# Shared network: seven blocks in the first route and one in retention's opening, gathers reordered, the last group power among block 0's scatters

## The reference, cut to what matters

```python
x = x + time_mix(layernorm(x))     # RWKV recurrence over time
x = x + ffn(layernorm(x))          # first expert layer
x = x + retention(layernorm(x))    # 16 heads, per batch of 1024 tokens
x = x + ffn(layernorm(x))          # second expert layer, the same weights
# ffn(x): 64 experts of 64 hidden, top 4 per token, weighted by a softmax
routed = einsum('ne,nef,efd->nd', comb, silu(x @ wg) * (x @ wu), wd)
shared = (silu(x @ swg) * (x @ swu)) @ swd     # 2 networks of 256 hidden
return routed + shared
# retention: scores = (q k^T) * decay, ret = scores v; group norm over a
# head's whole sequence; out = (silu(x wg) * norm(ret)) wo + bo
```

## Time and profile before

| what | value |
|---|---|
| median of 3 runs | 1552.0 us (1551.07 to 1554.17) |
| the profiled execution's own time | 1554.0 us |
| its span, first to last instruction | 1552.3 us |
| granted TensorE clock, mean | 0.911 of full |
| PE, DVE, POOL, ACT busy | 82%, 71%, 63%, 44% of the span |
| time_mix | up to about 184 us |
| moe1: route, expert pairs | to about 402 us, to about 600 us |
| retention: opening, rest | 604 to 692 us, to about 1005 us |
| moe2: route, expert pairs, sums | to about 1197 us, to about 1484 us, to 1552 us |

### The profile page before, as it was taken

One profiled execution on the slowest core, in us unless ns is written; L12 is line 12 of the kernel. 1 busy time (PEld: TensorE's weight loads), 2 busy tenths in 40 slices (PEclk: granted clock), 3 DMA queues, 4 the chain that ended last, 5 costly groups with the idle time before them and its releaser, 6 DMA issues. The chain is left out here.

```text
span 1552.3 us, 24686 instructions
## 1 busy us (share of the span) xinstructions
PE 1267.0 (82%) x7408; PEld 874.9 (56%) x7408; DVE 1098.7 (71%) x2756; ACT 687.5 (44%) x1464; POOL 984.6 (63%) x1308
## 2 busy tenths in 40 slices
PE   7788567998599997999898998389998887787751
PEld 3344444665488884556565766246655665665521
DVE  5899887776266664557687878567773777787758
ACT  6999421221366664234333441222211765665610
POOL 4999668888555554775665514287884566676710
PEclk9899768999799998999999899779999999999966
DMA  9900162223688786412021100182325655554178
GB/s 356 414 36 0 30 283 101 96 104 119 213 270 281 261 286 216 124 43 79 29 72 41 56 1 33 30 351 81 105 98 148 199 178 177 171 180 137 45 284 298
DMA packets 109399, 233.83 MB, mean 151 GB/s; under 512 B 21544, under 2 KB 43471, under 8 KB 108757
## 3 DMA queue, kind: packets, MB, share of 16 engines
q1 hardware_dynamic: 81076, 164.03, 31.6%
q0 software_dynamic: 27648, 68.23, 12.9%
q10 hardware_dynamic: 544, 0.00, 0.0%
HBM read 125.44 MB, written 115.11 MB: 155 GB/s over the span
## 5 line engine op out<-in xcount | busy, mean ns | idle before, releaser
L978 POOL DMA_INDIRECT slots_x<-arena,slot x240 | 250.5, 1044 | 42.9 <-POOL slot L931 33.4
L1342 POOL DMA_INDIRECT pairs_y<-arena x192 | 189.4, 986 | 109.4 <-DVE arena L1413 54.3
L762 PE MATMUL moe_wide<-arena 128*128 128x512 f32 x416 | 198.2, 623 | 17.7 <-DVE arena L1091 17.7
L1259 PE MATMUL moe_narrow<-arena 128*128 128x128 f32 x1536 | 211.2, 282 | 0.0
L1259 PEld LDWEIGHTS moe_narrow<-arena 128*128 128x128 f32 x1536 | 194.4, 199 | 1.5 <-issue 1.0
L1405 DVE TENSOR_TENSOR arena<-arena,moe_narrow 64x128 f32<-64x128 f32 x384 | 111.6, 291 | 103.9 <-ACT arena L1307 88.9
L484 POOL DMA_INDIRECT arena<-slots_y,slot x128 | 126.1, 985 | 82.7 <-DMA arena<-slots_y,slot 44.1
L1272 PE MATMUL moe_wide<-arena 64*128 64x256 f32 x768 | 125.2, 424 | 53.1 <-DVE arena L1405 51.9
L1301 ACT ACTIVATE arena<-moe_narrow 128x512 f32<-128x512 f32 x192 | 114.7, 597 | 95.6 <-PE moe_narrow L1248 92.4
L1413 DVE COPY arena<-moe_wide 128x512 f32<-128x512 f32 x192 | 128.3, 689 | 33.1 <-DMA pairs_y<-arena 27.7
L1248 PE MATMUL moe_narrow<-ident,arena 128*128 128x128 f32 x768 | 128.7, 293 | 21.7 <-DMA arena<-slots_x 21.7
(11 more groups left out here) (342 smaller groups left out, 2462.0 us busy)
## 6 DMA issues: line engine op xcount, KB each, us to landing
arena<-slots_x SPq DMA_DIRECT2D x192, 264.0 KB, 3.4
slots_x<-arena SPq DMA_DIRECT2D x48, 528.0 KB, 15.8
slots_y<-arena SPq DMA_DIRECT2D x96, 256.0 KB, 3.3
arena<-w_gu SPq DMA_DIRECT2D x2, 8192.0 KB, 28.8
arena<-pairs_y SPq DMA_DIRECT2D x32, 512.0 KB, 4.7
residual<-x SPq DMA_DIRECT2D x8, 512.0 KB, 8.6
arena<-sw_gu SPq DMA_DIRECT2D x4, 1024.0 KB, 6.0
slots_x<-arena,slot POOLq DMA_INDIRECT x256, 2.5
```

The source lines that it names most:

```text
L762: last = pe.matmul(bank[:, :], sgu[:, h, at:at + P], xnt[n % TRING][:, h, :], start=h == 0, stop=h == KH - 1)
L978: pool.indirect_dma_start(out=x_slots, in_=xn[:, t, :], in_offset=None, out_offset=bass.IndirectOffsetOnAxis(ap=slot[:, t, i:i + 1], axis=0))\
L1259: last = pe.matmul(h_ps[n % 2][:, j * P:(j + 1) * P], weights[:, n % 3, j, h, :], xt[:, n % XTRING, (j * KH + h) * P:(j * KH + h + 1) * P] ...
L1342: pool.indirect_dma_start(out=slots.y_of, in_=ytile[:, n % YRING, j, :], in_offset=None, bounds_check=slots.pairs - 1, oob_is_err=False, o ...
```

## The change

moe1's route computes the shared network of 7 blocks instead of 6, so retention's opening has one block of it instead of two (LATE is 1), and the lists of PE, ACT and DVE in the opening are written anew for one. POOL's list there has the first power behind the gathers of tiles 0 to 5 (before: 0 to 6), the second behind those of tiles 6 to 9 (before: 7 and 8), and decay_k and decay_q of the first half next to each other. scatter takes a range of its 16 transfers; the power for block 2 comes behind the fourth, the last group power behind the thirteenth. In moe2's route_scalar the table load moves from the head to behind the copies of block 2's transposes. The arithmetic and the number of instructions stay the same apart from where the seventh block is computed.

```diff
--- before.py
+++ after.py
@@ -832,9 +832,6 @@
             hand_over(pe, "slots")
 
         def route_scalar(act):
-            if first:
-                act.preload_act_table(ACT.Silu)
-
             def normalise(n):
                 act.wait_ge(sem("moments_ready"), n + 1)
                 shifts, scales = (first.offset, first.rstd) if n < SEEN else \
@@ -868,7 +865,10 @@
                 act.sem_inc(sem("xn_done"), BLK * DONE)
                 act.sem_inc(sem("lg_copied"), DONE)
                 normalise(2)
-                for n in (2, 0, 1):
+                keep_transposes(2, 0)
+                keep_transposes(2, 1)
+                act.preload_act_table(ACT.Silu)
+                for n in range(DONE):
                     keep_transposes(n, 0)
                     keep_transposes(n, 1)
                 keep_logits(2)
@@ -1853,12 +1853,13 @@
         pool.iota(self.xn[:, :, D + K:D + 2 * K], [[K * P, self.BLK * self.ROUTED], [1, K]], base=-self.k.slots.NOWHERE,
                   channel_multiplier=K, allow_small_or_imprecise_dtypes=True).then_inc(self.sem("first_numbers"), 1)
 
-    def scatter(self, pool):
-
-        pool.wait_ge(self.sem("first_numbers"), 1)
-        pool.wait_ge(self.sem("first_xn"), self.BLK)
-        pool.wait_ge(self.sem("first_slots"), 1)
-        for at in range(self.BLK * self.K):
+    def scatter(self, pool, transfers):
+
+        if 0 in transfers:
+            pool.wait_ge(self.sem("first_numbers"), 1)
+            pool.wait_ge(self.sem("first_xn"), self.BLK)
+            pool.wait_ge(self.sem("first_slots"), 1)
+        for at in transfers:
             t, i = at // self.K, at % self.K
             if at:
                 pool.wait_ge(self.landed[(at - 1) % 2], 16 * ((at + 1) // 2))
@@ -1951,14 +1952,14 @@
     LATE = NT // BLK - first_late
     SH = sw_d.shape[0] // P
     LQ = SH * LATE
-    assert LATE == 2 and 2 * SH * P == T
+    assert LATE == 1 and 2 * SH * P == T
     late_sgu = gates[:, :, T:2 * T]
     late_sd = arena.take(SH, D, at=masked_at + GR * 4 * P + P + W)
     assert P + W + SH * D <= 2 * GR * 4 * P - GR * 4 * P
     late_xn = arena.take(LATE, BLK, D, at=kst_at)
     late_xnt = arena.take(LATE, CH, N, at=decay_at)
     late_sg = arena.take(2, N, at=ret_at + CH * T - 2 * N)
-    late_sht = [qm[:, c, par, N:T] for c in range(CH) for par in range(2)] + [t[:, c, N:T] for t in (qst, kt) for c in range(CH)]
+    late_sht = [qm[:, c, par, N:T] for c in range(CH) for par in range(2)]
     assert len(late_sht) == LQ
     powers_dram = nc.dram_tensor("gamma_powers", (HEADS, W), F32, kind="Internal").ap()
 
@@ -2193,26 +2194,17 @@
 
             late_transposes(0)
             pe.wait_ge(sem("late_gu_w"), 16)
-            late_gate_up(0)
-            late_gate_up(1)
-            late_transposes(1)
-            for q in range(2, SH + 1):
+            for q in range(LQ):
                 late_gate_up(q)
             pe.wait_ge(sem("late_d_w"), 16)
             late_down(0, 0)
-            late_gate_up(SH + 1)
             late_down(0, 1)
-            for q in range(SH + 2, LQ):
-                late_gate_up(q)
-
-            pe.wait_ge(sem("late_hidden"), LQ - 1)
+
+            pe.wait_ge(sem("late_hidden"), LQ)
             transpose_x(0, 0, first=True)
             pe.wait_ge(sem("w_qk"), 16 * LOADS)
-            project(0, 0, range(CH))
-            late_down(1, 0)
-            project(0, 0, range(CH, 2 * CH))
+            project(0, 0, range(2 * CH))
             pe.wait_ge(sem("w_vg"), 16 * LOADS)
-            late_down(1, 1)
             project(0, 0, range(2 * CH, PJ_USES))
             transpose_x(0, 1, first=True)
             project(0, 1, range(PJ_USES))
@@ -2348,14 +2340,9 @@
 
             late_normalise(0)
             late_copy_xt(0)
-            late_normalise(1)
-            late_silu(0)
-            late_silu(1)
-            late_copy_xt(1)
-            for q in range(2, LQ - 1):
+            for q in range(LQ):
                 late_silu(q)
             normalise(0, 0)
-            late_silu(LQ - 1)
             copy_xt(0, 0, first=True)
             act.wait_ge(sem("parity"), 1)
             act.wait_ge(sem("w_qk"), 16 * LOADS)
@@ -2455,15 +2442,14 @@
 
             gather(0, range(2))
             constants()
-            gather(0, range(2, 7))
+            gather(0, range(2, 6))
             layernorm_power(0)
-            gather(0, [7])
-            gather(1, [0])
+            gather(0, range(6, 8))
+            gather(1, range(2))
             layernorm_power(1)
-            gather(1, [1])
+            gather(1, [2])
             pool.wait_ge(sem("decay"), 16 * 4 * CH)
             decay_k(0, 0)
-            gather(1, [2])
             decay_q(0, 0)
             gather(1, [3])
             decay_k(0, 1)
@@ -2495,9 +2481,11 @@
                     first.power(pool, powers_made, 0, 2)
             pool.wait_ge(sem("added"), 2 * choices.K * (TB // 2 * (B - 1) + BLK // 2))
             first.number_pairs(pool)
-            first.scatter(pool)
+            first.scatter(pool, range(4))
             first.power(pool, powers_made, 2, 3)
+            first.scatter(pool, range(4, 13))
             group_power(B - 1)
+            first.scatter(pool, range(13, BLK * choices.K))
 
         @block.vector
         def _(dve):
@@ -2642,11 +2630,9 @@
                                          powers[0:HEADS, P + m:P + m + 1], None, ALU.mult))
                 m *= 2
             dve.sem_inc(sem("powers"), 1)
-            late_multiply(0)
-            late_multiply(1)
+            for q in range(LQ):
+                late_multiply(q)
             add_choices(0, 0)
-            late_multiply(2)
-            late_multiply(3)
             dve.wait_ge(sem("blocks"), 3)
             c.link(dve.tensor_reduce(parity, blocks.rearrange("p (g q d) -> p q g d", q=2, d=DH)[:, :, :, 0], AX_X, ALU.add))
             dve.wait_ge(sem("w_qk"), 16 * LOADS)
@@ -2654,21 +2640,15 @@
                 c.step(dve.tensor_scalar(bias_m[:, m], parity, bias_t[:, 0, m:m + 1], None, ALU.mult))
             c.settled()
             dve.sem_inc(sem("parity"), 1)
-            late_multiply(4)
+            late_add(0, 0)
+            late_add(0, 1)
             add_choices(0, 1)
-            late_add(0, 0)
             statistics(0, 0)
-            late_multiply(5)
-            late_add(0, 1)
-            late_multiply(6)
             add_choices(0, 2)
-            late_multiply(7)
             add_choices(0, 3)
             statistics(0, 1)
-            late_add(1, 0)
-            late_add(1, 1)
+            keep_values(0, 0)
             add_choices(1, 0)
-            keep_values(0, 0)
             add_choices(1, 1)
             statistics(1, 0)
             keep_values(0, 1)
@@ -2804,7 +2784,7 @@
     with ExitStack() as ctx:
         k = Kept(nc, ctx)
         time_mix(nc, k, x, w_rvk, w_out, time_decay, time_first)
-        experts(nc, k, "moe1", 1, False, 6, 0, router_w, router_bias, w_gu, w_d, sw_gu, sw_d)
+        experts(nc, k, "moe1", 1, False, 7, 0, router_w, router_bias, w_gu, w_d, sw_gu, sw_d)
         first = retention(nc, k, w_qk, w_vg, w_o, b_q, b_k, b_vg, b_o, gn_w, gn_b, gamma, sw_gu, sw_d, router_w, router_bias, x.shape[0])
         experts(nc, k, "moe2", 2, True, 7, k.res.shape[1], router_w, router_bias, w_gu, w_d, sw_gu, sw_d, out=out, first=first)
```

## The result

The changed kernel takes 1558.43 us (median of 20 runs, 1554.27 to 1568.44), the kernel before, run beside it, 1552.84 (20 runs, 1544.06 to 1561.59). The ratio is 1.0043 with a 95% interval of 1.0026 to 1.0060: slower by 4 to 9 us, where 1550.6 was forecast with 1545.5 to 1556 as the range.

A forecast was written before the change was run, and what follows sets the result against it. Barriers between the program's blocks were taken to decide, by who reaches each last. 3.5 + 5.5 - 9.1 - 1.3 = -1.4 us on a median of 1552.0 gave 1550.6, range 1545.5 to 1556.

The forecast's parts named there:

- Part 3: Retention's end: group power behind the thirteenth scatter ends DVE's wait, -9.1 us.
- Rival 3: Retention's end: variance ready while POOL stands behind a late scatter, gain 2.7 less per scatter; chance 0.06 with rival 4.
- Part 2: Retention's opening: the later second power, behind sixteen paced gathers, makes PE stand and its clock fall, +5.5 us.
- Rival 1: Retention's opening nearly free because gathers are not paced, +0.1 to +2.6; total 1545.2 to 1547.7; chance 0.24.
- Part 1: First route: seventh block nearly fits PE's free time; PE and DVE replace POOL's scatters as its end, +3.5 us.
- 4.45: First route: how many us later the first expert load comes, priced from the second route's seven blocks.
- The credit of 1: Behind the first route's barrier: some 3 us less at half clock give Pe back about 1 us.
- bound of +5.5: First route: upper bound of the seventh block's cost, with PE's pause before block 6 costing one more us.
- rival 4: First route: seventh block costs its upper bound, total 1552.6 us; chance 0.06 with rival 3.
- 32.27: Second route: us from block 5's product to the last sum, copied to the first route, w_d loads included.
- Part 4: Second route's head: table load hidden where ACT waits for PE anyway, -1.3 us.
- rival 2: Retention's opening: slower gathers, 4.0 us for two, make it +10.3; total 1555.4 us; chance 0.14.

The follow-up runs named there:

- e1: The changed kernel itself, run and profiled again; 1.0038 of the kernel before.
- e2: The changed kernel with group power and table load put back, so moved block and gathers alone; 1.0090 of the kernel before.
- e18: The changed kernel with DVE's page naming moved behind block 5's product, on a chip like the first; 0.9972 of the kernel before.
- e11: The changed kernel with DVE's page naming moved behind block 5's product, on a slower chip; 0.9999 of the kernel before.
- e17: The kernel before with the new opening alone, six blocks in the first route, block 6's shared network left out; 1.0032 of the kernel before.
- e7: The changed kernel with six blocks in the first route, block 6's shared network left out; 0.9998 of the kernel before.
- e3: The kernel before with only the last group power moved behind the thirteenth scatter; 0.9944 of the kernel before.
- e9: The kernel before with seven blocks in the first route, block 6's shared network added twice, on a slower chip; 1.0066 of the kernel before.
- e16: The kernel before with group power amid the scatters and page naming behind block 5's product, on a slower chip; 0.9929 of the kernel before.
- e6: The changed kernel with the old order of gathers and powers in retention's opening; 1.0010 of the kernel before.
- e8: The changed kernel with the opening's second power ahead of the gathers of tiles 8 and 9; 1.0097 of the kernel before.
- e13: The kernel before with seven blocks in the first route, block 6's shared network added twice, on another slower chip; 1.0033 of the kernel before.
- e15: The changed kernel with page naming behind block 5's product, on another slower chip; 0.9964 of the kernel before.

## Why the prediction was wrong, step by step

- **Part 3, -9.1: right.** -9.09 in the pause (10.14 to 1.05), -8.7 us in the run of it alone, placed and priced as forecast. Rival 3 didn't occur.
- **Part 2, +5.5: right, mechanism and size.** The second power was forecast 666.5, 62.4 into the opening; it is 63.0 to 64.5. PE stood 10.25 to 10.72 us there and its clock fell, POOL's wait of 5 ahead of the first power measured 4.74 and 5.99, and the opening grew by 5.6 (e1, e2) to 7.5 in the longest run; alone, the part took +5.0. Rival 1 (the rule of the Trainium skill, "DMA: Bandwidth & Descriptors", section "Anatomy of one DMA - SWDGE (gpsimd) path", of some 2 us and the bytes for a gather) would have had the eight gathers unpaced. POOL's timeline of e1 has waits of 0.7 to 1.3 us ahead of every second one of them, and the eight took 13.3 us (663.2 to 676.5), against 13.2 forecast and 10.0 by the rule.
- **Part 1, +3.5: this step failed.** It measured +6.15 at the barrier. Two terms of it were wrong. The 4.45 was taken from one second route and left out that the clock may fall in the pause ahead of block 6's first group; the text saw this pause and priced it at one more us in the bound, and it costs 1.7 (5.37 less 3.68) and occurs in every first route with seven blocks. The credit of 1 for a shorter slow stretch behind the barrier is not seen: experts took 199.1 to 202.7 us with six blocks and 200.7 to 203.5 with seven. So the bound of +5.5 was too low as well, and rival 4 the right direction with too small a size. The overlap was wrong too: the text counted the last two loads of w_d as part of the 32.27, because the second route has them at the same place. There the scatters are over by then; here they hold the last scatter back by 6 us, to the very end of the route. POOL's scatters did not stop being the route's end, they tie with PE and DVE, and e18 and e11 show them holding the load once the other path is shorter.
- **Part 4, -1.3: not shown.** It is there at the route's head (-1.0), and the runs give -1.4 and +2.3 with intervals of some 4 us on either side.
- **Sum.** With the measured sizes it is 6.15 + 5.6 - 9.1 - 1.0 = +1.7, and the changed kernel is 5.6 us slower by the medians, 4 to 9 by the interval. Of the 7.0 us by which the forecast was off, Part 1 is 2.65 and parts 2 and 4 are 0.4; some 4 us stay open, and without them the time would have been in the range. e2 gives the same gap: 14.0 against 6.15 + 5.6 less the 2.4 by which its pause is shorter. By runs alone the route's half is 14.0 - 5.0 = 9.0 in one pair (e2 and e17) and 6.2 in the other (e1 and e7), each with 5 us on either side. The table hints where the rest lies: the batches are 286.5 to 290.8 us long in the six profiles with seven blocks (mean 289.0) and 285.5 to 287.1 in the six with six (mean 286.4), e7 and e17 with the new opening among these. So 2.6 us of batches, and 0.6 of experts by the same means, go with the seventh block and not with the opening. The code of the batches is the same in e1 and e7, the two slower chips show no such difference (294.4 to 299.1 and 296.9 to 300.8), and no run tests it: the cause is open.
- **Chances.** Faster and same had 0.84. The sum -1.4 held a credit of 1.3 for the table load that could only shrink, one of 1.0 for the clock, an estimate, and a term whose reason to be larger stood in the text. None of the three came out in the forecast's favour, and the chance of slower, 0.16, held rival 2 alone.

## What to carry over

A duration taken from another place of the same kernel includes the clock that was granted there: look for a pause of PE inside the copied stretch, and price it at both levels, from rows. Look also at what the DMA queues do in either place: here large weight loads were clear of the scatters in one route and on top of them in the other. Work that fills an idle engine isn't free if a third engine's chain then ends last (here DVE's page naming ahead of a product that PE waits for), and taking 21 us from an engine gains nothing where a DMA queue sets the end. A change of four parts can hold a good one: the group power amid the scatters alone (e3) is 0.56% faster than before; with the page naming moved it was 0.7% and 0.4% faster on the two slower chips.

## What the runs showed of the hardware

**Chips differ by 5%, and not evenly.** On two of the four chips that the experiments ran on the kernel before took 1618 and 1635 us instead of 1552. The stages before the first expert load are as long there as elsewhere (402.7 to 408.8, except e9's 420.2), and most of it is in the expert pairs of the second layer and what follows: 395 to 411 us in place of 350 to 359. In the opening one can see what such a loss looks like; rows of e16, ACT's and DVE's timelines and the windows of its opening, beside those of e3:

```profile
644.76 0.60 ACT L2281 ACTIVATE arena<-ret_sc 128x512 f32<-128x512 f32 x1 [12.05 <-DMA arena<-slots_expert]
...
645.39 0.69 DVE L2537 TENSOR_TENSOR arena<-arena,ret_sc 128x512 f32<-128x512 f32 x1 [11.48 <-issue]
...
606.00:708.00 102.00, 84.06 (x266) 47.80 (x266) 44.18 (x119) 34.40 (x58) 64.52 (x69) 0.90 0.36 106
```

```profile
603.00:692.40 89.40, 81.38 (x267) 46.42 (x267) 45.10 (x119) 34.40 (x58) 65.42 (x69) 0.95 0.40 121
```

The busy times are the same but for PE's, whose clock is lower. Most of the 12.6 us is a standstill of ACT, 12.05 where e3 has 2.84 ahead of the same activation, and its matmuls had ended 11 us before; the transfer that the row names as releaser belongs to the first route, so it isn't the cause, and what held ACT is not in the profile. A part of 5 us can come out differently on such chips (the opening alone: +5.0 on one kind, -0.6 and -3.1 on the other, each with 3 to 5 us on either side).

**A pause of 3 us can cost PE nothing or 1.7 us.** The same code with the same pause (2.85 to 3.03) went on at a granted clock of 1.00 in one execution of it and fell in another (rows of 3 us show 0.66 in e1's first route and 0.54 in the changed kernel's second), where 1.00 is 2.4 GHz and half of it 1.2. The eight matmuls behind it took 3.68 or 5.37 us. What PE had done before was alike: 16 matmuls without a gap in both.

**A scatter lands 4 to 6 us later when large loads are under way.** The last scatter of a route landed 2.2 to 2.5 us after its issue in all 20 second routes profiled and in the ten first routes with six blocks, where the loads of w_d were over or not yet issued. With 2 MB of such loads issued 1 to 6 us ahead of the scatter it took 6.5 to 8.7 (the changed kernel, e1, e2, e6, e8, e11, e13, e15, e18). In e9, seven blocks too, the loads came 7 us after the scatter, and it took 2.4.
